# Two typed layers of a graph network: tables stage and sum stage become one block

## The reference

```python
seg = concatenate([edge_type * n + src, (edge_type + R) * n + dst])      # R = 9 types, two directions
srcs = concatenate([dst, src])
for l in range(2):
    agg = segment_sum(output[srcs], seg, 2 * R * n)                      # per type, direction and node
    hidden = output @ W[-1] + b[-1]                                      # "own"
    for r in range(R):
        for inv in (0, 1):
            s = r + R * inv
            hidden = 2.0 * (hidden + agg[s] @ W[s] + count[s] * b[s]) / max(count[s], 1)
    output = relu(hidden) if l == 0 else hidden
```

## Time and profile before

| | us |
| --- | --- |
| median of 3 runs | 4357.26 |
| fastest and slowest | 4351.77, 4358.05 |
| profiled execution, span | 4864.0 |
| typed layers in it (first table matmul to second turning back) | 2185.4 to 4729.1 |
| layer 0: tables, sum | 2185 to 2394, 2394 to 3509 |
| layer 1: tables, sum | 3513 to 3725, 3725 to 4729 |
| granted TensorE clock, mean | 0.767 |

### The profile page before, as it was taken

One profiled execution on the slowest core, in us unless ns is written; L12 is line 12 of the kernel. 1 busy time (PEld: TensorE's weight loads), 2 busy tenths in 40 slices (PEclk: granted clock), 3 DMA queues, 4 the chain that ended last, 5 costly groups with the idle time before them and its releaser, 6 DMA issues. The chain is left out here.

```text
span 4864.0 us, 55522 instructions
## 1 busy us (share of the span) xinstructions
PE 3316.3 (68%) x16061; PEld 2560.9 (53%) x16062; DVE 2277.9 (47%) x3880; ACT 1443.0 (30%) x2832; POOL 1744.4 (36%) x1969
## 2 busy tenths in 40 slices
PE   6979775999997999897465555555764443333359
PEld 3545423689995969783254444444632333322257
DVE  8979996244545525564343333333434222221134
ACT  5848576456666636540000000000000000000005
POOL 0000012011110102016356656666064666666631
PEclk8989898999998999997655555565776656655569
DMA  3000056388884839555311111111053111111115
GB/s 140 0 1 0 7 200 219 143 272 291 290 291 151 293 139 310 176 199 208 126 40 46 46 39 44 46 46 45 30 178 117 47 46 46 47 46 48 47 44 189
DMA packets 161511, 570.70 MB, mean 117 GB/s; under 512 B 46177, under 2 KB 54722, under 8 KB 160909
## 3 DMA queue, kind: packets, MB, share of 16 engines
q1 hardware_dynamic: 89494, 394.83, 23.5%
q0 software_dynamic: 71408, 172.45, 11.9%
q10 hardware_dynamic: 390, 0.60, 0.0%
HBM read 405.06 MB, written 162.66 MB: 117 GB/s over the span
## 5 line engine op out<-in xcount | busy, mean ns | idle before, releaser
L2027 PE MATMUL ps_sum_rgcn<-gathered_rgcn,select_sum_rgcn 128*128 x3328 | 980.0, 426 | 649.2 <-issue 624.8
L2027 PEld LDWEIGHTS ps_sum_rgcn<-gathered_rgcn,select_sum_rgcn 128*128 128x128 f32 x3328 | 752.4, 294 | 732.3 <-issue 729.7
L1943 POOL DMA_INDIRECT gathered_rgcn<-by_dst,row x782 | 737.7, 943 | 405.3 <-issue 217.5
L1609 PE MATMUL ps_sum_arma<-pair_counts_f_sum_arma,parts_sum_arma 128*128 128x448 f32 (+1 forms) x3850 | 852.0, 373 | 13.6 <-ACT pair_counts_f_sum_arma L1650 13.6
L1609 PEld LDWEIGHTS ps_sum_arma<-pair_counts_f_sum_arma,parts_sum_arma 128*128 128x128 f32 x3850 | 708.1, 190 | 67.6 <-issue 14.2
L1943 POOL DMA_INDIRECT gathered_rgcn<-by_src,row x558 | 526.4, 943 | 393.0 <-issue 152.4
L2064 ACT COPY acc_rgcn<-ps_sum_rgcn 128x128 f32<-128x128 f32 x100 | 26.5, 265 | 2060.5 <-PE ps_sum_rgcn L2027 971.3
L2101 DVE TENSOR_TENSOR select_sum_rgcn<-one_hot_sum_rgcn,ps_coef_sum_rgcn 128x2048 f32<-128x2048 bf16 x52 | 118.9, 2287 | 755.1 <-PE ps_sum_rgcn L2027 391.8
L1488 POOL DMA_DIRECT2D rows<-parts_sum_arma x275 | 153.6, 559 | 882.6 <-DVE parts_sum_arma L1697 840.2
L1959 PE MATMUL ps_got_sum_rgcn<-factor_parts,turned_sum_rgcn 128*128 x832 | 181.9, 221 | 311.4 <-DVE turned_sum_rgcn L2078 241.8
L2078 DVE COPY turned_sum_rgcn<-ps_turn_sum_rgcn 128x1024 bf16<-128x1024 bf16 x104 | 71.7, 690 | 653.1 <-DMA params_norm_h<-in_L_gnn_beta 410.0
(11 more groups left out here) (459 smaller groups left out, 5173.7 us busy)
## 6 DMA issues: line engine op xcount, KB each, us to landing
blocks_arma_mid<-pairs SPq DMA_DIRECT2D x125, 800.0 KB, 6.3
axT_arma<-pairs SPq DMA_DIRECT2D x100, 800.0 KB, 5.7
pair_counts_arma_sum<-pairs SPq DMA_DIRECT2D x50, 800.0 KB
rows<-parts_sum_arma POOLq DMA_DIRECT2D x275, 128.0 KB, 5.4
by_src<-rows_rgcn_tables SPq DMA_DIRECT2D x50, 576.0 KB
by_dst<-rows_rgcn_tables SPq DMA_DIRECT2D x50, 576.0 KB
exact<-whole_pairs SPq DMA_DIRECT2D x25, 800.0 KB, 3.3
pairs<-whole_pairs POOLq DMA_DIRECT2D x25, 800.0 KB, 5.2
```

The source lines that it names most:

```text
L1609: last = nc.tensor.matmul(ps[:, g, 0:here.stop - here.start], half(part), counts[:, n % 2, here].bitcast(F32R), start=t == 0 and part == 0 ...
L1943: nc.gpsimd.indirect_dma_start(got[:, n % PLACES, :], None, table, bass.IndirectOffsetOnAxis(ap=o.row[:, n % C:n % C + 1], axis=0)).then_i ...
L2027: nc.tensor.matmul(ps[:, bass.ds(slot, P)], select[:, parity, u, :], rows[:, bass.ds(place, D)], start=False, stop=False, skip_group_check ...
```

## The change

Tables stage and sum stage of a layer become one block, `typed_layer_stage`, without the meeting of the engines between them. Its memory is shared in time: the row buffers of the tables and `select`, `turned` and `mine` of the sum lie in the same SBUF; all eight PSUM banks are one tile, used as 5 + 3 by the tables and as 2 + 1 + 2 + 2 by the sum. Waits take the place of the meeting. On each engine the table work stands ahead of the sum work, in program order:

- POOL issues all gathers in one loop; gathers 112 to 127 have no wait ahead of them any more. Before gather 416 (the first that reads `by_dst`) it waits for all 50 tiles.
- PE waits for all adds and own rows before it touches the sum's banks.
- DVE waits for its own adds, makes the first one-hots, and waits for the stores' landing before it writes the shared SBUF.
- ACT relays all 50 stores, then waits for the own rows, then seeds.
- SP stores, in layer 0 waits for the own rows and loads the next weights, then counts landings.

The turning back of layer 0 moves into the block of layer 1, ahead of its tables: PE's 25 transposes first, then the table matmuls, each of the first five, and each first of a bank's four tiles, behind ACT's eviction of that bank. The turning back of layer 1 stays a stage.

```diff
-def typed_sum_stage(nc, k, tag, tables, got, acc, find, loads=()):
+def typed_layer_stage(nc, k, tag, xT, tables, got, acc, find, turned_from=None, loads=()):
...
     with Stage(nc, tag) as c:
+        shared = c.sb("rows_then_select", [P, J * R * D])
+        table_rows = shared[:, :].rearrange("p (j f) -> p j f", j=J)
         hot = c.sb("one_hot", [P, 2, U, P], BF16)
-        select = c.sb("select", [P, 2, U, P])
+        ends = [2 * U * P, 2 * U * P + OCTET * P, 2 * U * P + OCTET * P + U * PARTS * R]
+        select = shared[:, 0:ends[0]].rearrange("p (h u f) -> p h u f", h=2, u=U)
...
+        room = c.psum("room", [P, 8, SPAN])
+        ps_table, ps_own = room[:, 0:J, :], room[:, J:8, :]
+        ps = room[:, 0:2, :].rearrange("p b f -> p (b f)")
...
         @block.sync
         def _(sp):
+            sp.wait_ge(k.filled, 16)
+            for v in range(TILES):
+                order, t = divmod(v, NT)
+                sp.wait_ge(drained, M * v + M)
+                sp.dma_start(tables[order][t * P:t * P + P, :], table_rows[:, v % J, :]).then_inc(stored[v % J], 16)
+            if loads:
+                sp.wait_ge(own_biased, FOURS)
             for to, source in loads:
...
         @block.gpsimd
         def _(gp):
-            for n in range(EARLY, TOTAL * U):
...
+            for n in range(U):
+                gp.wait_ge(tiled, (needs[n] & COUNTS))
+                nc.gpsimd.nop(nofuse=True)
+                for lane in range(LANES):
+                    gather(lane * U + n)
+            gp.wait_ge(tiled, NT)
+            for n in range(BEHIND, TOTAL * U):
                 if not fetched(n):
                     continue
+                if n == C:
+                    gp.wait_ge(tiled, TILES)
                 if n == PLACES:
...
             nc.tensor.sem_inc(multiplied, U)
+            if turned_from is not None:
+                for t in range(NT):
+                    last = nc.tensor.transpose(room[:, t // 4, t % 4 * P:t % 4 * P + P], acc[:, t, :], k.ident[:, :])
+                    if t % 4 == 3 or t == NT - 1:
+                        last.then_inc(flopped, 1)
+            for v in range(TILES):
+                order, t = divmod(v, NT)
+                for part in range(M):
+                    m = v * M + part
+                    s = order * R + part * PARTS
+                    if m >= J:
+                        pe.wait_ge(drained, m - J + 1)
+                    if turned_from is not None:
+                        if m < J:
+                            pe.wait_ge(turned_back, m + 1)
+                        elif v < NT and t % 4 == 0 and part == 0:
+                            pe.wait_ge(turned_back, t // 4 + 1)
...
+            pe.wait_ge(drained, TILES * M)
+            pe.wait_ge(own_biased, FOURS)
             pe.wait_ge(zeroed, 1)
...
+            if turned_from is not None:
+                for g in range(FOURS):
+                    here = slice(g * 4 * P, min(g * 4 * P + 4 * P, NP))
+                    act.wait_ge(flopped, g + 1)
+                    nc.scalar.activation(xT[:, here], room[:, g, 0:here.stop - here.start], turned_from).then_inc(turned_back, 1)
+            for v in range(TILES):
+                act.wait_ge(stored[v % J], 16 * (v // J + 1))
+                nc.scalar.sem_inc(tiled, 1)
+            act.wait_ge(own_scaled, FOURS)
             act.wait_ge(opened, 1)
...
+            dve.wait_ge(drained, TILES * M)
             nc.vector.tensor_copy(ps_iota[:, 0:P], k.iota[:, 0:P]).then_inc(shown, 1)
...
             heat(0, 0)
             if find:
                 heat(U, 1)
+            for j in range(J):
+                dve.wait_ge(stored[j], 16 * (TILES // J))
+            if find:
                 for g in range(3):
...
-        for layer, xT in ((0, k.xT[:, :]), (1, hidden)):
-            typed_tables_stage(nc, k, f"rgcn_tables{layer}", xT, [dram["by_src"], dram["by_dst"]], got, acc)
-            typed_sum_stage(nc, k, f"sum_rgcn{layer}", typed, got, acc, layer == 0,
-                            loads=() if layer else typed_loads(k, A, 1))
-            turn_back_stage(nc, k, f"rgcn_back{layer}", acc, hidden, ACT.Copy if layer else ACT.Relu)
+        tables = [dram["by_src"], dram["by_dst"]]
+        typed_layer_stage(nc, k, "sum_rgcn0", k.xT[:, :], tables, got, acc, True, loads=typed_loads(k, A, 1))
+        typed_layer_stage(nc, k, "sum_rgcn1", hidden, tables, got, acc, False, turned_from=ACT.Relu)
+        turn_back_stage(nc, k, "rgcn_back1", acc, hidden, ACT.Copy)
```

More of the change, by code:

```diff
@@ L655, in late @@
     return range(max(u - LAG, 0), u + 1) if u == U - 1 else range(u - LAG, u - LAG + 1) if u >= LAG else ()
[L660 to L750, removed]
-                    dve.wait_ge(own_biased, g + 1)
-                    nc.vector.tensor_tensor(acc[:, tiles, :], acc[:, tiles, :],
-                                            own_factor[:, tiles, None].to_broadcast([P, n, P]), ALU.mult).then_inc(own_scaled, 1)
-        @block.scalar
-        def _(act):
-            for t in range(NT):
-                act.wait_ge(stored[t % J], 16 * (t // J + 1))
-                nc.scalar.sem_inc(tiled, 1)
-        @block.sync
-        def _(sp):
-            sp.wait_ge(k.filled, 16)
-            for v in range(TILES):
-                order, t = divmod(v, NT)
-                sp.wait_ge(drained, M * v + M)
-                sp.dma_start(tables[order][t * P:t * P + P, :], rows[:, v % J, :]).then_inc(stored[v % J], 16)
-            for j in range(J):
-                sp.wait_ge(stored[j], 16 * (TILES // J))
@@ L1874, in ring_lists @@
         nc.vector.tensor_scalar(items[:, :, :, 0], steps(tile_of[:, n, :]), float(SPAN), None, ALU.mult)
-def typed_sum_stage(nc, k, tag, tables, got, acc, find, loads=()):
+def typed_layer_stage(nc, k, tag, xT, tables, got, acc, find, turned_from=None, loads=()):
     Q = U // 4
+    M = R // PARTS
+    W = PARTS * D
+    FOURS = -(-NT // 4)
+    OWN = 8 - J
+    w, bias, own_factor = k.typed_w, k.typed_bias, k.factor[:, :, 0]
+    typed = [table.rearrange("n (r f) -> (n r) f", f=D) for table in tables]
+    TILES = len(tables) * NT
     ORDERS = len(tables)
@@ L1929, in _, with gather @@
         def _(gp):
-            for n in range(EARLY, TOTAL * U):
+            def gather(n):
+                nc.gpsimd.indirect_dma_start(
+                    got[:, n % PLACES, :], None, typed[n // C],
+                    bass.IndirectOffsetOnAxis(ap=k.orders[n // C].row[:, n % C:n % C + 1], axis=0)).then_inc(
+                        arrived[n % PLACES // GROUP], 16)
+            needs = nc.values_load_multi_w_load_instructions(
+                k.need[0:1, 0:U], engines=(mybir.EngineType.Pool,), min_val=1, max_val=NT,
+                skip_runtime_bounds_check_because="counts of tiles, at least one")[1]
+            for n in range(U):
[5 more added lines that the diff above has]
+            for n in range(BEHIND, TOTAL * U):
                 if not fetched(n):
                     continue
+                if n == C:
+                    gp.wait_ge(tiled, TILES)
                 if n == PLACES:
@@ L1941, in _ @@
                         nc.gpsimd.nop(nofuse=True)
[L1942 to L1946 removed]
+                gather(n)
         @block.tensor
```

61 lines of the change are left out of this document (48 added, 13 removed).

## The result

Median 4326.74 us (4311.34 to 4328.04, 4 runs) against 4357.66 us for the kernel before beside it (4351.77 to 4359.1, 4 runs): ratio 0.9931, 95% interval 0.9915 to 0.9947. The change gains 30.9 us, 23 to 37 by the interval.

A forecast was written before the change was run, and what follows sets the result against it. POOL's gathers, one per 1.249 us, were taken to bound the typed layers. Seams 1.4, layer 0's waits 8.9 and turning back 1.7 sum to 12.0 us gained: 4357.3 to 4345 us, range 4328 to 4356.

The forecast's parts named there:

- the seam's own part: Between tables and sum, POOL's join with about 0.4 us of draining and signals: 0.7 us a layer, 1.4 in both, goes.
- My check: Timed run leaves 2037 us for layers and surroundings; POOL-bound layers sum to 2000, slow tables to 2092, too long.
- the slow stretches: Tables and sums of the first profile: PE and DVE slow beside gathers, taken as the recording's doing, absent from timed runs.
- PE's late start in layer 0: Seam of layer 0: POOL's waits at gathers 128 (0.9 us) and 160 (8.0 us) both go, 8.9 us gained.
- Turning back: Between the layers: first table matmul straight behind the 25 transposes, at 3511.6 instead of 3513.28, gaining 1.7 us.
- Costed at nothing: ACT's relays, SP's order, DVE's store waits, POOL's wait before gather 416 and semaphore clears (under 1 us) add no time.
- The wait at gather 128: Sign in the profile after: POOL has no idle time before gather 112 but a wait at gather 128.
- A: Rival: seam idle in timed runs too, tables really slow beside gathers; 22 us gained, 4335 us; chance 0.15.
- B: Rival: PE is quick and gather 160 in layer 0 hardly waits; 6 us or less gained, 4352 us; chance 0.22.
- C: Rival: PE, not POOL, bounds layer 0 in timed runs, its start 45 us earlier counts fully; 4312 us; chance 0.05.
- D: Rival: gathers get longer in the merged block, 0.961 instead of 0.944 us costing 26.6 us; 4372 us; chance 0.09.
- E: Rival: DVE's copies hold gathers up where they newly meet; 7.4 us gained, 4350 us; chance 0.03.

The follow-up runs named there:

- second profile of before: The kernel before, with no edit, profiled once more: 4351.15 us, one run, span 4349.8 us.
- Layer 0 alone: Against the kernel before, tables and sum in one block in layer 0 only, layer 1 and turning back unchanged: ratio 0.9955 (0.9941 to 0.9968).

## Why the prediction was wrong in size

- **The step that failed: the seam's own part, "about 0.4 of draining and signals", 0.7 us a layer.** It measures 9.8. Both layers together, this is 18.2 us too little. The forecast lacked 18.9: its other terms were 2.3 too high, and 3.0 are not placed, which is within the interval. No row carried that 0.4, and its bound from above should have been the idle time of the rows at that place, 44.2 and 48.1 us, nearly all of which I gave the slow tables. A drain ahead of a join hides behind whatever engine is later; in a profile whose tables were slow, it could not be seen at all, and in the timed runs POOL was the last engine and it stood bare.
- **My check had a gap that size.** The layers and what lies around the span had 2037 us, and my account filled 2000. I used it only to rule out 2092. Of the 37 us open, 18 were these two drains; two more drains, at the layers' ends, reach 2.8 us past the last take-out each. Some 13 stay open.
- **That the slow stretches are the recording's**: right in what it was used for, since the timed runs have quick tables: both later profiles have a time of their own and tables of 103 us. What made the first profile slow is not shown; its execution has no time of its own.
- **PE's late start in layer 0, 8.9 us**: right in place, 6.9 in the second profile of before; in the kernel with layer 1 alone merged it is 9.9 (1.2 at gather 128, 8.7 at 160), so it varies by execution. The forecast's 8.0 at gather 160 lies between 5.9 and 8.7. That is partly luck: 12 items at 12.3 us for 16 take 9.2 us, not 9.5, and a step takes 13.4 us in the changed kernel, not 14.1.
- **Turning back, 1.7**: 1.4. The table matmul came 4.4 us behind the first transpose, not 2.8, because the transposes run at a lower granted clock, 0.63, than those of the earlier trace rows, 1.00. The separate stage pays the same in the second profile of before (0.64). A slip of 0.1: 25 transposes of 2.92 us end at 3511.7, not 3511.6.
- **Costed at nothing** (relays, SP's order, gather 416's wait, clears): nothing seen; from the first gather of a layer on, none starts more than 1.72 us behind the last.
- **Signs.** The wait at gather 128 that the prediction named as a sign did not come; its own sum had it gone. Layer 0 alone gained 19.6 us, and its interval reaches past the 20 named as a sign of being wrong.
- **Rivals.** A: wrong, since POOL does not wait for the tables; its 22 us came nearer than my 12 for another reason. B: wrong, the wait at gather 160 is 5.9 to 8.7, not 2.3. C: wrong, PE waits 587.7 us for landed gathers in the changed kernel. D: wrong, 0.944. E: wrong; the only longer gathers, up to 1.408 us, lie in 2247 to 2281 and 3250 to 3284, beside the tables and ahead of the first copy; those beside the copies stay at 0.961 us at most, and the 125 that overlap a copy have the mean of the others, 0.944. The rule of the Trainium skill (SBUF — State Buffer, "Who interferes with whom") is about copies in a two-port mode. These read PSUM, and no run shows which mode they ran in, so this is no test of the rule, and the 4.6 us that the prediction drew from it rest on a mode that nobody had shown.

## What to carry to other kernels

A join drains each engine, and on the engine that bounds the kernel that drain is bare: price it by where that engine comes to the join, not by when its last instruction ends, and put work of other engines beside it where the join must stay. When a profile is disturbed, a long idle time in it can hide a cost at that place, up to its own length; here 44 and 48 us hid 9.8. When an account is meant to close, what it leaves open is the next thing to price, not proof enough that the other account is worse.

## What the runs showed of the hardware

- A POOL drain behind indirect gathers costs 2.1 us behind 1 to 4 of them and 8.9 to 9.7 behind 112 or more, although the last gather's rows had landed: the last items, which read them, start 2.2 us behind the last gather's end, and the drain ends 7 us later, with no DMA packet in between. What it waits for, no run tells.
- POOL's sequencer (the part that reads the instructions and hands them on) runs 12 gathers, 15.2 us, ahead of the gathers as recorded; a semaphore raised behind a gather is no sign that it ran.
- One profile of a kernel was 506.7 us too long with PE and DVE slow beside gathers; the thirteen profiles that followed, among them one of the same kernel, were not. What made it so is not shown.
- Executions of one kernel differ by up to 22 us (4342.7 to 4364.32 in 12 runs), and the stages ahead of the typed layers, the same in all these kernels, by up to 17: the first table matmul starts at 2174.4 in one profile and at 2191.3 in another. Sums by place in a profile tell 1 to 10 us apart where the times don't.
